# A batched landmark solve: matrices placed in SBUF by the stage in front, no masks, shorter pivot steps, right sides in a tile of their own

## The reference, cut to what matters

```python
Q, K, V = heads(query @ Wq.T + bq), heads(query @ Wk.T + bk), heads(query @ Wv.T + bv)
landmarks = K[:, :, landmark_idx, :]              # 64 indices 0, 16, 32, ... ; clamped to 0..31
Phi_Q = exp(-sq_dists(Q, landmarks) / temperature)
Phi_K = exp(-sq_dists(K, landmarks) / temperature)
W_kernel = Phi_K[:, :, landmark_idx, :] + 1e-6 * eye(64)
Y    = solve(W_kernel, einsum('bhnk,bhnd->bhkd', Phi_K, V))
norm = max(Phi_Q @ solve(W_kernel, Phi_K.sum(-2)), 1e-10)
out  = (Phi_Q @ Y / norm) -> heads joined -> @ Wo.T + bo
```

## Time and profile before

| | us |
|---|---|
| three runs | 5329.72, 5331.76, 5329.89 (median 5329.89) |
| profiled execution: its time / its span | 5331.69 / 5329.8 |
| chunks of `kernel_matrices` in the span | about 1640 to 1876 |
| `landmark_solve`, first DMA issue to the issue of the result's store | 1876.1 to 2060.4 |
| VectorE busy in 1876.0 to 1954.4, and in 1954.4 to 2060.4 | 31.08, 75.04 |
| mean granted TensorE clock of the whole span | 0.862 |

### The profile page before, as it was taken

How to read it: one execution, slowest core, us unless ns; L and a number is a source line. 1 busy time by engine, 2 the same in 40 slices (tenths; PEclk the granted TensorE clock), 3 DMA queues, 4 the chain that set the end, 5 groups by cost and what they waited for, 6 DMA issues and landing times. The chain is left out here.

```text
span 5329.8 us, 94009 instructions
## 1 busy us (share of the span) xinstructions
PE 4033.8 (76%) x34138; PEld 3002.4 (56%) x34138; DVE 3060.2 (57%) x5339; ACT 1994.1 (37%) x3780; POOL 727.0 (14%) x808
## 2 busy tenths in 40 slices
PE   7999999999975602799945659899994137867476
PEld 5777777777753402576633236576773025655364
DVE  2555555555556654422235456577777964867673
ACT  2333333333334500233323334366664324653322
POOL 0000000000011101100002026500002133210420
PEclk7999999999998855899976769899997568989567
DMA  2111111111111272100020023212220000000000
GB/s 72 49 48 46 43 48 48 48 44 44 48 30 60 80 91 72 60 0 0 0 50 5 0 81 128 83 58 62 58 66 7 0 5 3 0 11 1 7 0 20
DMA packets 251779, 209.82 MB, mean 39 GB/s; under 512 B 84288, under 2 KB 241952, under 8 KB 244256
## 3 DMA queue, kind: packets, MB, share of 16 engines
q1 hardware_dynamic: 251552, 206.80, 13.6%
HBM read 181.54 MB, written 24.95 MB: 39 GB/s over the span
## 5 line engine op out<-in xcount | busy, mean ns | idle before, releaser
L3362 PE MATMUL c_psO<-c_pt,c_vc 128*128 128x512 f32 x1024 | 482.1, 593 | 2.5 <-ACT c_ot L3449 2.5
L3334 PE MATMUL c_psS<-c_kc,c_qt 128*128 128x257 f32 x2048 | 465.9, 380 | 0.9 <-issue 0.9
L3334 PEld LDWEIGHTS c_psS<-c_kc,c_qt 128*128 128x128 f32 x2048 | 381.2, 190 | 66.8 <-issue 17.4
L3488 DVE COPY c_qt<-c_psQ 128x512 f32<-128x512 f32 x248 | 170.8, 689 | 399.7 <-PE c_psQ L3319 399.7
L3441 ACT ACTIVATE c_sc<-c_psS,c_mx 128x257 f32<-128x257 f32 x512 | 215.2, 473 | 486.8 <-DVE c_mx L3499 486.8
L508 PEld LDWEIGHTS f_psY<-f_w_down,f_hT 128*128 128x128 f32 x2560 | 302.3, 192 | 64.3 <-issue 50.4
L498 PE MATMUL f_psH<-f_xs,f_w_up 128*128 128x512 f32 x640 | 310.1, 621 | 18.4 <-ACT f_hT L551 18.4
L551 ACT ACTIVATE f_hT<-f_psH,f_b_up 128x512 f32<-128x512 f32 x320 | 215.0, 688 | 288.9 <-PE f_psH L498 284.1
L3319 PEld LDWEIGHTS c_psQ<-XT,c_m 128*128 128x128 f32 x1984 | 260.1, 191 | 106.2 <-issue 104.4
L508 PE MATMUL f_psY<-f_w_down,f_hT 128*128 128x128 f32 x2560 | 305.4, 275 | 10.3 <-ACT f_hT L551 7.1
L615 DVE SCALAR_TENSOR_TENSOR X<-f_psY,f_wt,X 128x128 f32 x256 | 72.1, 345 | 379.8 <-PE f_psY L508 379.8
(11 more groups left out here) (710 smaller groups left out, 8269.4 us busy)
## 6 DMA issues: line engine op xcount, KB each, us to landing
c_kc<-in_ctxT SPq DMA_DIRECT2D x128, 257.0 KB, 3.3
c_vc<-in_ctx SPq DMA_DIRECT2D x128, 256.0 KB
g_wide<-g_w_dram SPq DMA_DIRECT2D x32, 1024.0 KB, 7.8
x_kc<-in_ctxT SPq DMA_DIRECT2D x32, 512.0 KB, 3.8
x_vc<-in_ctx SPq DMA_DIRECT2D x64, 256.0 KB
l_k_dram<-l_dist SPq DMA_DIRECT2D x32, 256.0 KB, 2.9
l_q_dram<-l_turn SPq DMA_DIRECT2D x8, 1024.0 KB, 3.9
s_A<-l_k_dram SPq DMA_DIRECT2D x32, 256.0 KB, 5.9
```

The costliest lines, as they stand in the source:

```text
L3334: mm = pe.matmul(psS[:, r, 0:KEYS], qt[:, b // BT, half, b % BT, r * G:(r + 1) * G].rearrange("p h i -> p (h i)"), kc[:, b // 2 % 2, b % 2 ...
L3362: mm = pe.matmul(psO[:], vc[:, slot, c % 2, t, half * P:(half + 1) * P], pt[:, c % 2, t], start=(t == 0), stop=(t == 1))
```

## The change

`A` becomes a tile `l_A` of shape 32 x 16 x 32 per partition that exists from before `kernel_matrices`. SyncE, whose loop over chunks is now written out, moves the matrices of a chunk from `k_dram` to the 16 partitions of its sequences with one DMA (`place`), issued one chunk later, between the stores of `dist[:, 0]` and of `turn`; the last `place` stands behind the last right sides, and the stage ends only when it has landed (`k_placed`). In `landmark_solve` the 32 loads, the mask multiplications and the copy of the right sides into `A` are gone; steps of tokens that are no landmark are still skipped. `eliminate` works on parts of `PART` = 8 rows, from each part's first column on, with the pivot row saved in `col` as the multipliers (it uses that the matrix is symmetric). The right sides stay in `rr` and are updated apart, 16 rows at a time. Rows that are no landmark are set to zero once, at the end.

```diff
-    kernel_matrices(k, q_dram, k_dram, r_dram)
-    landmark_solve(k, k_dram, r_dram, y_dram, REG, NL, J)
+        A = sb("l_A", [P, S, H16, S])
+        kernel_matrices(k, q_dram, k_dram, A, r_dram)
+        landmark_solve(k, A, r_dram, y_dram, REG, NL)
...
-                with sp.Fori(0, CHUNKS) as i:
+                def place(i):
+                    sp.wait_ge(k_stored, (i + 1) * TC * 16)
+                    sp.dma_start(A[i * BC:(i + 1) * BC].rearrange("b i h j -> b (i h j)"),
+                                 k_dram[i * TC:(i + 1) * TC].rearrange("t (b i) r c -> (t b) (i r c)", b=BT))\
+                        .then_inc(k_placed, 16)
+                for i in range(CHUNKS):
                     sp.wait_ge(exp_done, i * 2 + 1)
                     for t in range(TC):
...
+                    if i:
+                        place(i - 1)
                     sp.wait_ge(turned, i + 1)
...
+                place(CHUNKS - 1)
                 sp.wait_ge(q_stored, 16 * CHUNKS)
-                sp.wait_ge(k_stored, 16 * TILES)
+                sp.wait_ge(k_placed, 16 * CHUNKS)
...
-                for i in range(S):
-                    sp.dma_start(A[:, i, :, 0:S],
-                                 k_dram.rearrange("t (b i) r (q j) -> (t b) i (r q) j", b=BT, q=4)[:, i])\
-                        .then_inc(rows_loaded[i // ROWS], 16)
...
-                ln(v.tensor_tensor(pair[:], bcast(land[:], 1, S), bcast(land[:], 2, S), ALU.mult))
-                for n in range(S // ROWS):
-                    v.wait_ge(rows_loaded[n], 16 * ROWS)
-                    part = slice(n * ROWS, (n + 1) * ROWS)
-                    ln(v.tensor_tensor(A[:, part, :, 0:S], A[:, part, :, 0:S], bcast(pair[:, part], 2, H16), ALU.mult))
-                v.wait_ge(rr_loaded, 16)
-                ln(v.tensor_tensor(A[:, :, :, S:J],
-                                   rr[:].rearrange("p i (h d) -> p i h d", d=V),
-                                   bcast(bcast(land[:], 2, H16), 3, V), ALU.mult))
...
                     ln(v.tensor_scalar(piv[:], A[:, n, :, n], diag[:, n:n + 1], None, ALU.add))
                     ln(v.reciprocal(piv[:], piv[:]))
-                    ln(v.tensor_tensor(A[:, n, :, n + 1:J], A[:, n, :, n + 1:J], bcast(piv[:], 2, J - n - 1),
-                                       ALU.mult))
-
-                    for lo, hi in ((n + 1, min(S, n + 1 + S // 2)), (n + 1 + S // 2, S)):
-                        if lo >= hi:
-                            continue
-                        m = hi - lo
-                        ln(v.tensor_tensor(tmp[:, 0:m, :, n + 1:J], bcast(A[:, lo:hi, :, n], 3, J - n - 1),
-                                           bcast(A[:, n, :, n + 1:J], 1, m), ALU.mult))
-                        ln(v.tensor_tensor(A[:, lo:hi, :, n + 1:J], A[:, lo:hi, :, n + 1:J],
-                                           tmp[:, 0:m, :, n + 1:J], ALU.subtract))
+                    ln(v.tensor_tensor(rr[:, n], rr[:, n], bcast(piv[:], 2, V), ALU.mult))
+                    ln(v.tensor_copy(col[:, :, n + 1:S], A[:, n, :, n + 1:S]))
+                    ln(v.tensor_tensor(A[:, n, :, n + 1:S], A[:, n, :, n + 1:S], bcast(piv[:], 2, W), ALU.mult))
+                    for lo in range(n + 1, S, PART):
+                        hi = min(S, lo + PART)
+                        part = tmp[:, 0:hi - lo, :, lo:S]
+                        by = bcast(col[:, :, lo:hi].rearrange("p h i -> p i h"), 3, S - lo)
+                        ln(v.tensor_tensor(part, by, bcast(A[:, n, :, lo:S], 1, hi - lo), ALU.mult))
+                        ln(v.tensor_tensor(A[:, lo:hi, :, lo:S], A[:, lo:hi, :, lo:S], part, ALU.subtract))
+                    for lo in range(n + 1, S, 2 * PART):
+                        hi = min(S, lo + 2 * PART)
+                        part = tmp_r[:, 0:hi - lo]
+                        by = bcast(col[:, :, lo:hi].rearrange("p h i -> p i h"), 3, V)
+                        ln(v.tensor_tensor(part, by, bcast(rr[:, n], 1, hi - lo), ALU.mult))
+                        ln(v.tensor_tensor(rr[:, lo:hi], rr[:, lo:hi], part, ALU.subtract))
...
-                v.tensor_copy(rr[:].rearrange("p i (h d) -> p i h d", d=V), A[:, :, :, S:J]).then_inc(solved, 1)
+                v.tensor_tensor(rr[:], rr[:], bcast(bcast(land[:], 2, H16), 3, V), ALU.mult).then_inc(solved, 1)
```

More of the change, by code:

```diff
@@ L2476, in layer0_attn, with kernel_matrices @@
     q_dram = nc.dram_tensor("l_q_dram", (CHUNKS, P, G * CHUNK), F32).ap()
-    kernel_matrices(k, q_dram, k_dram, r_dram)
-    landmark_solve(k, k_dram, r_dram, y_dram, REG, NL, J)
+    ctx = Stage(k)
+    with ctx:
+        sb, _ = buffers(nc, ctx)
+        A = sb("l_A", [P, S, H16, S])
+        kernel_matrices(k, q_dram, k_dram, A, r_dram)
+        landmark_solve(k, A, r_dram, y_dram, REG, NL)
     landmark_read(k, q_dram, y_dram)
-def kernel_matrices(k, q_dram, k_dram, r_dram):
+def kernel_matrices(k, q_dram, k_dram, A, r_dram):
     nc = k.nc
@@ L2759, in landmark_solve @@
     RUN = 4
+    PART = 8
     ctx = Stage(k)
@@ L2762, in landmark_solve @@
         sb, ps = buffers(nc, ctx)
-        A = sb("s_A", [P, S, H16, J])
-        rr = sb("s_rr", [P, S, H16 * V])
-        tmp = sb("s_tmp", [P, S // 2, H16, J])
+        rr = sb("s_rr", [P, S, H16, V])
+        tmp = sb("s_tmp", [P, PART, H16, S])
+        tmp_r = sb("s_tmp_r", [P, PART * 2, H16, V])
+        col = sb("s_col", [P, H16, S])
         idx_i = sb("s_idx_i", [P, NL], I32)
@@ L2813, in _ @@
                 ln(v.tensor_scalar(cnt[:], cnt[:], 1.0, None, ALU.max))
-                ln(v.reciprocal(cnt[:], cnt[:]))
-                ln(v.tensor_scalar(cnt[:], cnt[:], REG, -1.0, ALU.mult, ALU.add))
-                ln(v.tensor_tensor(cnt[:], cnt[:], land[:], ALU.mult))
-                ln(v.tensor_scalar(diag[:], cnt[:], 1.0, None, ALU.add))
-                ln(v.tensor_tensor(pair[:], bcast(land[:], 1, S), bcast(land[:], 2, S), ALU.mult))
-                for n in range(S // ROWS):
-                    v.wait_ge(rows_loaded[n], 16 * ROWS)
-                    part = slice(n * ROWS, (n + 1) * ROWS)
-                    ln(v.tensor_tensor(A[:, part, :, 0:S], A[:, part, :, 0:S], bcast(pair[:, part], 2, H16), ALU.mult))
-                v.wait_ge(rr_loaded, 16)
-                ln(v.tensor_tensor(A[:, :, :, S:J],
-                                   rr[:].rearrange("p i (h d) -> p i h d", d=V),
-                                   bcast(bcast(land[:], 2, H16), 3, V), ALU.mult))
+                ln(v.reciprocal(diag[:], cnt[:]))
+                ln(v.tensor_scalar(diag[:], diag[:], REG, None, ALU.mult))
                 ln(v.tensor_copy(land_i[:], land[:]))
@@ L2847, in substitute @@
-                def substitute(n):
-                    for lo, hi in ((0, min(n, S // 2)), (S // 2, n)):
-                        if lo >= hi:
-                            continue
-                        m = hi - lo
-                        ln(v.tensor_tensor(tmp[:, 0:m, :, S:J], bcast(A[:, lo:hi, :, n], 3, V),
-                                           bcast(A[:, n, :, S:J], 1, m), ALU.mult))
-                        ln(v.tensor_tensor(A[:, lo:hi, :, S:J], A[:, lo:hi, :, S:J], tmp[:, 0:m, :, S:J],
-                                           ALU.subtract))
+                    ln(v.tensor_tensor(rr[:, n], rr[:, n], bcast(piv[:], 2, V), ALU.mult))
@@ new lines, in eliminate @@
+                    if W == 0:
+                        return
+                    ln(v.tensor_copy(col[:, :, n + 1:S], A[:, n, :, n + 1:S]))
[6 more added lines that the diff above has]
+                        ln(v.tensor_tensor(A[:, lo:hi, :, lo:S], A[:, lo:hi, :, lo:S], part, ALU.subtract))
@@ new lines, in eliminate @@
+                    for lo in range(n + 1, S, 2 * PART):
[4 more added lines that the diff above has]
+                        ln(v.tensor_tensor(rr[:, lo:hi], rr[:, lo:hi], part, ALU.subtract))
+                def substitute(n):
+                    for lo in range(0, n, 2 * PART):
+                        hi = min(n, lo + 2 * PART)
+                        part = tmp_r[:, 0:hi - lo]
+                        ln(v.tensor_tensor(part, bcast(A[:, lo:hi, :, n], 3, V), bcast(rr[:, n], 1, hi - lo), ALU.mult))
+                        ln(v.tensor_tensor(rr[:, lo:hi], rr[:, lo:hi], part, ALU.subtract))
```

18 lines of the change are left out of this document (7 added, 11 removed).

## The result

The changed kernel takes **5291.35 us** (median of 4 runs, 5285.4 to 5293.27) against 5330.23 (5329.72 to 5331.76, 4 runs) before, a ratio of 0.9925 [0.9908, 0.9942]: faster by 0.75%. The forecast was 5285 in a range of 5259 to 5302. The profiled execution took 5290.35 us, its span is 5288.5.

The account below looks back on a forecast made before the run. The solve was taken as one chain, loads then VectorE, which waited for 32 loads and idled at branches. From 5331.69 us, -73.6 in the solve and +26.7 for the added DMA gave 5284.8, forecast 5285, range 5259 to 5302.

Parts of the forecast that it names:

- The clock: Stage in front: TensorE's clock falls during the right sides, +1.6 us a chunk, +10 for six, 5295 us; chance 0.10.
- Up to the first pivot: Start of the solve: first pivot 12.7 us behind the stage's first issue instead of 78.3, -65.6 us.
- The steps: Solve: `eliminate(0)` -9.8 us to 33.6, `eliminate(16)` -0.6 to 12.9, final multiplication instead of a copy +2.4.
- The branches: Solve: VectorE's idle stretches over skipped steps keep their cost despite longer `eliminate` bodies, 0 us.
- the bound of +7: Solve: upper bound on the branches if ten more instructions cost 0.5 us on each of 14 skips.
- stretches that grow with the bodies: Solve: idle stretches at pivots should stay 7.3 and 8.0 us; growth with the bodies would show the prediction wrong.
- The middle chunks: Stage in front: `place` delays right sides' stores and ScalarE's third copy by 1.7 us in six chunks, +10.2 us.
- The last chunk: Stage in front, last chunk: `place` and `turn` delay the first right sides' store from 1870.05 to 1877.0, +6.9 us.
- the last place: End of the stage in front: the barrier waits for the final `place`, 11.1 us behind its issue, +9.6 us.
- Place's rate: DMA onto 16 partitions: half the 64 and 32 partition rates, 104 to 119 GB/s, reckoned as 9.6 us.
- the forecast case: Whole kernel: `place` takes 8.8 to 10.1 us, giving 5277 to 5292 us with the branches' bound; chance 0.62.
- A landing below 5 us or over 15: `place` into `l_A`: forecast to land some 10 to 13 us after issue; outside 5 to 15 would be wrong.

Follow-up runs that it names:

- e8_one_part: Changed kernel with the parts of 8 rows undone, all rows below the pivot in one product from the first column: 5304.56 us, ratio 0.9954.
- e2_place_behind: Changed kernel with each `place` issued behind the right sides' stores of its own chunk: 5274.96 us, ratio 0.99.
- e3_spread: Changed kernel with `place` filling every eighth partition instead of 16 neighbours, the result leaving in 8 DMAs: 5272.02 us, ratio 0.9889.
- e4_three_steps: Changed kernel without the tests over skipped steps, calling steps 0, 16 and 31 directly: 5261.01 us, ratio 0.9868.
- e7_loop_only: Kernel before the change with only SyncE's loop over chunks written out: 5324.34 us, ratio 0.9995.
- e5_late_parts: Changed kernel without `place`: four DMAs in the solve load the matrices by rows, each step waiting only for its rows: 5259.5 us, ratio 0.9866.

## Why the prediction was right

It was right in its main mechanisms and in its sign; the size is 6 us off at the median. Between the profiled executions the stage in front cost 7.7 us more than forecast and the solve gained 1.1 less. That makes 8.8, of which 3.2 were made up by chance, in the stages that nothing touches. The clock, a rival at 0.10, came true in part.

*Up to the first pivot, -65.6.* Measured -65.8, shown by the timeline.

*The steps, -9.8, -0.6 and +2.4.* Measured 33.67 us for 33.6, 12.92 for 12.9, and 4.96 for the last multiplication. One line for all tensor_tensor forms held down to 784 elements (974 ns for 975) and, in e8_one_part, up to 15376. e8_one_part also shows the parts at their work: without them the two steps take 12.3 us more. That is more than the 10.4 they gained, because the change also adds small instructions.

*The branches, 0.* Measured +1.3, since 7.26 became 8.30 and 8.02 became 8.32; inside the bound of +7 but not nothing. The prediction named stretches that grow with the bodies as a sign of being wrong, and one did grow, by 1.0 us. It counted only jumps in them; the traces show instruction fetches there too, and one more of them in each of the two stretches than before (e8_one_part).

*The middle chunks, +10.2.* The step that was mis-sized: +16.1. Of it 2.0 us or a little more a chunk, so 12 of the six, is the queue, where 1.7 was predicted, and here two errors stood against each other. `place` took 8.9 to 9.4 us and not 9.6. But the store of `turn` behind it, taken as 2.3 us from one window of one us, takes 2.7 before and 3.8 to 4.2 here: it begins while some of the engines are still at `place`, and the first right sides' stores run beside its end. It was through only at 1698.76, and ScalarE's third copy came at 1699.63, 17.82 us behind the chunk's first issue instead of 15.62. The other 4 us are the rival with the clock, which came true in three of the six chunks. Two chunks in the changed kernel's timeline, and a window on the token projections (L2607) of each:

```profile
1699.63 0.72 ACT L2686 ACTIVATE l_rb<-l_psR 32x288 f32<-32x288 f32 x2 [2.33 <-DMA l_r_dram<-l_rb]
...
1700.20 1.20 PE L2635 MATMUL l_psR<-l_vm,l_dist 128*32 128x36 f32 x32 [2.07 <-ACT l_rb L2686]
...
1731.35 0.72 ACT L2686 ACTIVATE l_rb<-l_psR 32x288 f32<-32x288 f32 x2 [2.55 <-DMA l_r_dram<-l_rb]
...
1731.92 1.27 PE L2635 MATMUL l_psR<-l_vm,l_dist 128*32 128x36 f32 x32 [2.29 <-ACT l_rb L2686]
1733.12 4.56 PE L2607 MATMUL l_psA<-l_w_tok,l_xs 128*128 128x384 f32 x8
```

```profile
1701.00:1703.00 2.00, 1.90 (x18) 1.00 (x14) 0.64 (x2) 0.76 (x2) 0.00 (x0) 1.00 0.26 62
1733.00:1735.00 2.00, 2.00 (x7) 1.22 (x5) 0.19 (x1) 0.48 (x2) 0.00 (x0) 0.50 0.30 71
```

TensorE stood for some 2 us ahead of the fourth tile in both; in the one the granted clock stayed at 1.00 (2.4 GHz), in the other it fell to 0.50 (1.2 GHz), and the projections took 4.56 us instead of 3.18, 1.4 more where the rival had 1.6. The prediction's argument against it, that the wait lies between two tiles, did not hold. With `place` moved or quicker there is no such wait, and the chunks of e2_place_behind and e3_spread run at 29.5 us. Why it hits some chunks and not others is open. It is not every second one as a rule: three kernels have `place` at this spot, the changed one, e4_three_steps and e8_one_part, and in the last the first, second, third and sixth of the six middle chunks are slow ones, at 33.0 to 33.3 us. Over the 18 chunks, waits of 1.96 to 2.21 us left the clock at 1.00 eight times, and waits of 2.03 to 2.31 were followed by 0.50 ten times, so the length of this wait alone does not decide it.

*The last chunk, +6.9, and the last place, +9.6.* Measured +7.7 and +10.5. The last `place` lands 11.8 us after its issue, where I had 1.2 + 9.6 + 0.3 = 11.1: its packets take 9.65 us, as forecast, but the landing is signalled 1.1 us behind the last of them and not 0.3.

*Place's rate.* Taken between two rows, 104 to 119 GB/s; measured 109 to 118, inside. No row gave the step from 32 partitions to 16 as a half, so this was a guess that came out, and half of 205 is 102.5 GB/s (10.2 us) rather than 104. With the bound of +7 on the branches the forecast case would reach 5296 and not 5292. A landing below 5 us or over 15 did not come.

*Not costed:* SyncE's loop written out, about -1 us (e7_loop_only).

What the prediction did not ask is whether the load had to move at all. Its largest term, -65.6, joins three things: the masks, 32 loads becoming one or a few, and the load's place. e5_late_parts keeps the first two, loads late but in the order of use, and has the same 13 us to the first pivot. The masks and the many small loads were the cost, not the hour of the load. No run tells these two apart. In the timeline of before the last mask begins when the last load has landed:

```profile
1943.22 4.42 DVE L2822 TENSOR_TENSOR s_A<-s_A,s_pair 128x4096 f32<-128x4096 f32 x1 [9.42 <-DMA s_A<-l_k_dram]
```

Behind the loads came only this mask (4.42 us) and the copy of the right sides (4.96); the other masks lay between the waits for loads.

## What to carry to other kernels

A load that is late because it is cut into many small DMAs should first be made large and ordered by use in its own stage; only what is still waited for then is worth a place in an earlier one. Before a DMA is put into a queue that a loop's stores go through in order, its drain time for just these partitions has to fit the gap that is open there: here 5.2 us fitted and 9 did not, and what stuck out was paid in every chunk, in half of them with a slower TensorE clock on top. And a long transfer can hold up an engine that does not wait for it, if that engine's next instructions are fetched behind it.

## What the runs showed of the hardware

- 1 MiB onto 16 neighbouring partitions drains in 8.9 to 9.65 us (109 to 118 GB/s) in the changed kernel, onto every eighth partition in 5.1 to 5.7 (183 to 206 GB/s); 8 MiB onto all 128 partitions go at 416 GB/s.
- A wait of some 2 us on TensorE (1.96 to 2.31) was followed by a granted clock of 0.50 in 10 of 18 chunks and left it at 1.00 in 8.
- With a DMA of 64 KB packets in flight, a fetch of 16 KB of instructions began 16.1 us behind the one before instead of 7.6 to 9.2, and TensorE stood for 6.6 us in its loop's first pass until 1.2 us behind the fetch; with that DMA elsewhere the wait was 0.8 us (one execution each).
- On VectorE, the tests around 32 steps, 29 of them skipped, cost 32.9 us over the two passes, with seven instruction fetches of 8 KB in it; the stretch before the second pivot is 7.26 to 7.37 us with two fetches in it and 8.30 to 8.48 with three.
